# Cross attention with layer norm on one core: score products over stacked high and low parts of q

## The chip, the core and the metric

One NeuronCore of a Trainium2 chip runs the whole kernel. The metric is device time in microseconds (us); lower is better. TensorE (PE) has weight loads recorded apart from its products (PEld). The other engines are VectorE (DVE), ScalarE (ACT), GpSimd (POOL) and SyncE (SP), which here only issues DMAs.

## What is computed

x is 4 x 2048 x 512, the context 4 x 77 x 512, all float32, and there are 16 heads of 32.

```python
qs = (x @ wq) in heads;  ks, vs = (ctx @ wk), (ctx @ wv) in heads
scores = qs . ks / sqrt(32);  scores = where(mask, -inf, scores)
attn = softmax(scores) @ vs
out = attn @ wo + x
result = (out - mean) / sqrt(var + 1e-5) * gamma + beta
```

## The kernel before

The 8192 rows of x make 64 tiles t of 128 rows, and 16 blocks of 4 tiles. The weights, x and q are each split into a high part, rounded to fp32r by ScalarE's copy, and a low part, the rest. A product of two split numbers is made of three fp32r matmuls: high by high, high by low, low by high.

q is projected transposed, a block at a time and in four pieces of 128 columns of wq: `project_q(i)` gives, for block i // 4, the q of the four heads of group i % 4 (12 matmuls of 512 columns, line 287). ScalarE copies the high part out of PSUM into `qh` (`keep_q`), VectorE subtracts for the low part `ql` (`low_q`, line 579). `kh` and `kl` hold k as a block diagonal over four heads: 128 contraction rows (4 heads x 32) by 4 x 77 = 308 columns.

`scores(t, groups)` (line 303) makes for each of a tile's four groups three matmuls of 308 columns, which add up in one PSUM bank; stationary are `qh`, `qh`, `ql`, moving `kh`, `kl`, `kh`. `mask_max` (lines 591 and 597) adds the mask and takes the row maximum, `exps` (451) is ScalarE's exponential, `row_sums` (604, 606) VectorE's sum and reciprocal, `normalise` (742, 744) GpSimd's product, `transpose_p` (313, 315) turns the weights round on TensorE, `keep_pt` copies them out, `weigh_v` (335) multiplies with v once for two or four tiles, `keep_a` and `low_a` split the result, `project_o` (348) multiplies with wo (12 matmuls of 512 columns), and `residual`, `deviation`, `standardise` and `gain_and_shift` make the layer norm. `score` work of tile t and output work of tile t - 5 (`LAG`) share an iteration.

Each engine's program is written out in order by hand, and semaphores join them. TensorE's iteration t is: scores of groups 0 and 1; a projection (of o, or of q in the tiles in `SECOND`, t = 5, 9, 13 and so on, where `weigh_v` follows); the transposes of tile t - 1, first half; scores of groups 2 and 3; the other projection; in the tiles in `FIRST` a `weigh_v`; the transposes, second half. q(t + 4) is projected in iteration t. Each MATMUL of the program has a weight load of its own.

SyncE issues every DMA in one order: context, wk, wq and slices of x (`load_slice`; 64 slices of 256 KB through the three buffers of `xraw`), then wv, mask, slices, wo, the first residual tiles, gamma, beta, mask, slices. In iteration t it loads slice t + 10, places v at t = 1 and t = 3 (`place_v`, ten DMAs each, lines 205 and 209), stores tile t - 7 (242) and loads a residual tile (193). A wait of one of these holds up all behind it. Opening work of VectorE that matters: `low_k` makes `kl`, one group at a time.

## Time and profile before

| | |
|---|---|
| median of 3 runs | 662.82 us (661.82 to 666.81) |
| the profiled execution | 661.71 us, of which the span is 659.7 us |
| granted TensorE clock, mean over the span | 0.993 |
| busy share of the span | PE 96%, PEld 74%, DVE 81%, ACT 77%, POOL 74% |
| DMA | 57.78 MB, mean 88 GB/s |

The span runs from the first to the last instruction; the profiled execution's own time is 2.0 us longer than that. Matmuls are pipelined and the ends of their records are modelled, so a record of one lasts longer than the next one is away: the distance from start to start, or the piece in the chain divided by its count, is what one costs.

### The profile page before, as it was taken

To read this page: it belongs to the slowest core of one execution; us is meant where nothing else is said; L and a number is where in the kernel's file an instruction comes from. 1 tells how busy PE (TensorE), PEld (TensorE's weight loads), DVE (VectorE), ACT (ScalarE), POOL (GpSimd) and SP (SyncE) were. 2 spreads that over 40 slices of the span, in tenths; PEclk is the share of its full clock that TensorE was granted. 3 is DMA by queue.
4 is the path that set the end of the run, shared out by engine and by line. 5 is a ranking of instruction groups with operands and counts; after the bars stand their busy time and mean duration, and the time that the engine had idled before them with its cause. 6 is when DMAs were issued, how large, how long until landed. Compare 5 with 4: busy or idle time off the path is not lost.

```text
span 659.7 us, 13001 instructions
## 1 busy us (share of the span) xinstructions
PE 630.9 (96%) x4096; PEld 488.7 (74%) x4096; DVE 531.1 (81%) x1010; ACT 510.4 (77%) x1560; POOL 488.5 (74%) x631
## 2 busy tenths in 40 slices
PE   7979899999999999999999999999999999998883
PEld 5647687786878778687878778786877868785762
DVE  5766778788879878887888978887887988787886
ACT  4677888797887878797888879788887878788650
POOL 6334449696986969697896969698796969577663
PEclk9989999999999999999999999999999999999998
DMA  8542112221232313221232222122221222111214
GB/s 259 199 119 51 44 43 90 78 96 65 97 106 81 96 48 105 89 97 65 81 107 94 73 76 96 66 96 98 79 97 64 84 79 65 49 49 65 80 34 143
DMA packets 36563, 57.78 MB, mean 88 GB/s; under 512 B 8592, under 2 KB 9616, under 8 KB 36496
## 3 DMA queue, kind: packets, MB, share of 16 engines
q1 hardware_dynamic: 36496, 56.96, 25.8%
q8 instruction: 34, 0.56, 0.3%
q14 instruction: 33, 0.27, 0.1%
HBM read 39.53 MB, written 16.78 MB: 85 GB/s over the span
## 4 chain that ended last, share of the span: by engine, by line
PE 80%; DVE 10%; ACT 4%; DMA 2%; issue 2%; SPq 1%; POOL 1%; POOLq 0%; DVEq 0%; ACTq 0%
PE bank L348 23%; PE bank L287 23%; PE bank L303 14%; PE bank L313 8%; PE bank L335 8%; DMA xraw<-xT 2%; ACT pr L451 2%; PE bank L315 2%; DVE pr L591 2%; DVE sm L604 1%; DVE nm L597 1%; DVE st L625 1%; PE bank L271 1%; ACT kh L474 1%; DVE pf L570 1%
## 5 line engine op out<-in xcount | busy, mean ns | idle before, releaser
L451 ACT ACTIVATE pr<-pr,nm 128x77 f32<-128x77 f32 x1024 | 269.9, 347 | 70.9 <-DVE nm L597 70.2
L742 POOL TENSOR_TENSOR pn<-pr,rec 128x512 f32<-128x512 f32 x128 | 135.0, 1054 | 113.8 <-DVE rec L606 106.0
L591 DVE SCALAR_TENSOR_TENSOR pr<-msk,bank 128x308 f32<-128x308 uint8 x256 | 109.4, 468 | 44.4 <-PE bank L303 44.3
L604 DVE TENSOR_REDUCE sm<-pr 128x8 f32<-128x616 f32 x128 | 99.3, 776 | 11.2 <-ACT pr L451 11.0
L597 DVE TENSOR_REDUCE nm<-pr 128x8 f32<-128x616 f32 x128 | 101.8, 795 | 4.4
L287 PE MATMUL bank<-xh,wqh 128*128 128x512 f32 x256 | 102.6, 401 | 1.9 <-DVE ql L579 1.3
L348 PE MATMUL bank<-woh,ah 128*128 128x512 f32 x256 | 101.6, 397 | 0.1
L348 PE MATMUL bank<-woh,al 128*128 128x512 f32 x256 | 101.3, 396 | 0.0
L348 PE MATMUL bank<-wol,ah 128*128 128x512 f32 x256 | 101.1, 395 | 0.0
L287 PE MATMUL bank<-xh,wql 128*128 128x512 f32 x256 | 100.6, 393 | 0.0
L287 PE MATMUL bank<-xl,wqh 128*128 128x512 f32 x256 | 100.2, 392 | 0.0
L734 POOL TENSOR_TENSOR xl<-xraw,xh 128x512 fp32r<-128x512 f32 x64 | 83.6, 1309 | 20.8 <-ACT xh L420 20.8
L420 ACT ACTIVATE ptr<-bank 128x512 f32<-128x512 f32 (+1 forms) x256 | 95.5, 426 | 3.4 <-PE bank L313 3.4
L313 PEld LDWEIGHTS bank<-ident,pn 128*128 128x128 f32 x512 | 60.6, 140 | 48.7 <-issue 24.5
L303 PE MATMUL bank<-kh,qh 128*128 128x308 f32 x256 | 88.7, 346 | 1.5 <-DVE ql L579 0.9
L313 PE MATMUL bank<-ident,pn 128*128 128x128 f32 x512 | 78.7, 276 | 9.2 <-ACT ptr L420 5.9
L303 PE MATMUL bank<-kh,ql 128*128 128x308 f32 x256 | 78.1, 305 | 0.0
L303 PE MATMUL bank<-kl,qh 128*128 128x308 f32 x256 | 78.0, 305 | 0.0
L768 POOL TENSOR_TENSOR y<-y,bet 128x512 f32<-128x512 f32 x56 | 72.8, 1299 | 4.4
L766 POOL TENSOR_TENSOR y<-y,gam 128x512 f32<-128x512 f32 x56 | 72.5, 1294 | 0.0
L579 DVE TENSOR_TENSOR ql<-bank,qh 128x512 fp32r<-128x512 f32 x64 | 43.8, 684 | 32.7 <-ACT qh L420 32.6
L467 ACT ACTIVATE y<-z,rs 128x512 f32<-128x512 f32 x56 | 46.0, 821 | 22.7 <-POOL rs L761 22.3
(63 smaller groups left out, 1083.9 us busy)
## 6 DMA issues: line engine op xcount, KB each, us to landing
xraw<-xT SPq DMA_DIRECT2D x64, 256.0 KB, 3.0
xres<-x SPq DMA_DIRECT2D x64, 256.0 KB, 2.6
out<-y SPq DMA_DIRECT2D x56, 256.0 KB, 2.0
wk_sb<-wk SPq DMA_DIRECT2D x4, 256.0 KB, 4.6
wq_raw<-wq SPq DMA_DIRECT2D x4, 256.0 KB, 5.9
wv_sb<-wv SPq DMA_DIRECT2D x1, 1024.0 KB, 6.3
wo_raw<-wo SPq DMA_DIRECT2D x1, 1024.0 KB, 6.4
out<-wv_sb SPq DMA_DIRECT2D x4, 256.0 KB, 3.7
```

The lines of the kernel that those rows point to most:

```text
L287: last = nc.tensor.matmul(o[:], w[:, k, m * P:(m + 1) * P], s[:, blk % 2, k, :], start=(n == 0), stop=(n == 3 * KT - 1))
L303: last = nc.tensor.matmul(o, w[blk % 2][:, g, r * P:(r + 1) * P], s[:, g, t // TB, :], start=(n == 0), stop=(n == 2))
L313: last = nc.tensor.transpose(PTB[0][:, s * P:(s + 1) * P], pn[:, half, s, :], ident[:])
L348: last = nc.tensor.matmul(o[:], w[:, k, r * P:(r + 1) * P], s[:, k, :], start=(n == 0), stop=(n == 3 * KT - 1))
L420: return nc.scalar.activation(dst, src, ACT.Copy)
L451: last = nc.scalar.activation(s, s, ACT.Exp, bias=nm[:, t % 2, h:h + 1], scale=1.0)
L591: nc.vector.scalar_tensor_tensor(out=pr[:, 4 * g:4 * g + 4, :], in0=msk[:, b % 2, t % TB, :].unsqueeze(1).broadcast_to([P, 4, LK]), scalar ...
L597: nc.vector.tensor_reduce(nm[:, t % 2, HH * half:HH * half + HH], pr[:, HH * half:HH * half + HH, :], AX.X, ALU.max, negate=True).then_inc ...
L604: nc.vector.tensor_reduce(sm[:, t % 2, hs], pr[:, hs, :], AX.X, ALU.add).then_inc(v_sum, 1)
L734: nc.gpsimd.tensor_tensor(xl[:, n // KT % 2, n % KT, :], xraw[:, n % NX, :], xh[:, n // KT % 2, n % KT, :].bitcast(f32), ALU.subtract).the ...
L742: nc.gpsimd.tensor_tensor(pn[:, half, 0:4, :].rearrange("p s (e k) -> p (s e) k", e=2), pr[:, hs, 0:KM], rec[:, t % 2, hs].unsqueeze(2).br ...
L768: nc.gpsimd.tensor_tensor(y_of(o), y_of(o), bet[:], ALU.add).then_inc(g_y, 1)
```

## The change

The scores are formed for two heads at a time. The 128 contraction rows hold the high part of q for a pair of heads (64 rows) and its low part (64 rows), in the new tiles `qx`; `kh` and `kl` hold k for a pair (2 x 77 = 154 columns) in both halves of the rows. A group is then two pairs by (`kh`, `kl`), four matmuls of 154 columns, 616 in place of 3 x 308 = 924; low by low is now in the sum too. DMAs move the rows: `pair_k` copies k to the other half of the rows (8 DMAs once), `stack_q` puts the two parts of each q piece in place (4 DMAs of 64 rows x 2 KB for each of 64). ScalarE and VectorE write q's parts into two-slot buffers (`qth`, `qtl`; the first four pieces into `ptr`) and wait with piece i for the stacking of piece i - 2.

q is projected one piece earlier (`q_early`, `q_late`: q(t + 5) from t = 3 on). The first eight slices of x have buffers of their own; the wo load, the residual loads and the split of wo (now in four parts, iterations 1 to 4) come later; `project_v(0)` goes ahead of the first scores and `project_v(1)` between the two halves; ScalarE's `exps(0, 0)` goes ahead of its work on slice 8.

The diff, cut, with eight leading blanks of each line taken away:

```diff
+PW = 2 * LK
...
+def q_early(t):
+    return (7,) if t == 3 else (t + 5,) if t in SECOND else ()
+def q_late(t):
+    return () if t < 0 or t in SECOND or t >= T - 5 else (t + 4,) if t < 3 else (t + 5,)
...
-kh = sb("kh", [P, NG, NB, GW], f32r)
-kl = sb("kl", [P, NG, NB, GW], f32r)
+kh = sb("kh", [P, NG, 2, NB, PW], f32r)
+kl = sb("kl", [P, NG, 2, NB, PW], f32r)
...
 xraw = sb("xraw", [P, NX, D])
-xh = sb("xh", [P, 2, KT, D], f32r)
-xl = sb("xl", [P, 2, KT, D], f32r)
+with ExitStack() as split:
+    xh = split.enter_context(nc.sbuf_tensor("xh", [P, 2, KT, D], f32r))
+    xl = split.enter_context(nc.sbuf_tensor("xl", [P, 2, KT, D], f32r))
+zt = sb("zt", [P, 4 * KT, D])
...
 ptr = sb("ptr", [P, 2, 5, D])
+qth = sb("qth", [P, 2, D], f32r)
+qtl = sb("qtl", [P, 2, D], f32r)
+qx0 = sb("qx0", [P, NG, 2, D], f32r)
...
+qx1 = sb("qx1", [P, NG, 2, D], f32r)
...
-qh, ql = (qh0, qh1), (ql0, ql1)
...
+qx = (qx0, qx1)
+def x_of(n):
+    return (xraw[:, n] if n < NX else ptr[:, 0, 4, :] if n < KT else wo_raw[:, n - KT, :] if n < 2 * KT
+            else xraw[:, (n - 2 * KT) % NX])
+def x_arrived(n):
+    return (d_x[n], 16) if n < 2 * KT else (d_xt[(n - 2 * KT) % NX], 16 * ((n - 2 * KT) // NX + 1))
+def q_temp(i):
+    rows = (ptr[:, 0, i, :].bitcast(f32r), ptr[:, 1, i, :].bitcast(f32r)) if i < 4 else (qth[:, i % 2, :], qtl[:, i % 2, :])
+    return rows
 def z_of(o):
-    return z[:, o % 2] if o < VFIN else wv_sb[:, o - VFIN] if o < VFIN + KT else xraw[:, o - VFIN - KT]
+    return z[:, o % 2] if o < VFIN else zt[:, o - VFIN]
...
+d_kd, d_qx = [sem(f"d_kd{i}") for i in range(2)], [sem(f"d_qx{m}") for m in range(NG)]
+d_x = [sem(f"d_x{n}") for n in range(2 * KT)]
...
 misc = [("q", i) for i in range(4)]
 for t in range(T):
     o = [("o", t - LAG)] if t >= LAG else []
-    q = [("q", t + 4)] if t + 4 < T else []
-    misc += q + o if t in SECOND else o + q
+    misc += [("q", i) for i in q_early(t)]
+    misc += o if t not in SECOND else []
+    misc += [("q", i) for i in q_late(t)]
+    misc += o if t in SECOND else []
 misc += [("o", o) for o in range(T - LAG, T)]
...
     def load_slice(n):
-        if n >= NX:
-            sp.wait_ge(g_xl, n - NX + 1)
-        sp.dma_start(xraw[:, n % NX, :], xT[n // KT, :, n % KT, :]).then_inc(d_xt[n % NX], 16)
+        if n >= 2 * KT:
+            sp.wait_ge(g_xl, n - NX + 1 if n >= 2 * KT + NX else n - 2 * KT + 1)
+        sp.dma_start(x_of(n), xT[n // KT, :, n % KT, :]).then_inc(x_arrived(n)[0], 16)
...
+    def pair_k(g):
+        for k, done in ((kh, a_k), (kl, v_k)):
+            sp.wait_ge(done, 4 * g + 8)
+            for u in range(2):
+                here, there = slice(64 * u, 64 * u + 64), slice(64 - 64 * u, 128 - 64 * u)
+                sp.dma_start(k[there, g:g + 2, u].rearrange("p g b k -> p g (b k)").bitcast(f32),
+                             k[here, g:g + 2, u].rearrange("p g b k -> p g (b k)").bitcast(f32)
+                             ).then_inc(d_kd[g // 2], 16)
+    def stack_q(i):
+        blk, m = i // 4, i % 4
+        if blk >= 2:
+            sp.wait_ge(p_s, 4 * NG * (blk - 1))
+        sp.wait_ge(a_qh, i + 1)
+        for u in range(2):
+            rows = slice(64 * u, 64 * u + 64)
+            sp.dma_start(qx[blk % 2][rows, m, u].bitcast(f32), q_temp(i)[0][rows].bitcast(f32)).then_inc(d_qx[m], 16)
+        sp.wait_ge(v_ql, i + 1)
+        for u in range(2):
+            here, there = slice(64 * u, 64 * u + 64), slice(64 - 64 * u, 128 - 64 * u)
+            sp.dma_start(qx[blk % 2][there, m, u].bitcast(f32), q_temp(i)[1][here].bitcast(f32)).then_inc(d_qx[m], 16)
     for k in range(KT):
         sp.dma_start(wq_raw[:, k, :], w_v(wq)[:, k, :]).then_inc(d_wq[k], 16)
         load_slice(k)
     sp.dma_start(wv_sb[:], w_v(wv)).then_inc(d_wv, 16)
-    load_mask(0)
     for n in range(4, 8):
         load_slice(n)
+    load_mask(0)
+    pair_k(0)
+    stack_q(0)
+    stack_q(1)
+    pair_k(2)
+    stack_q(2)
+    stack_q(3)
+    load_mask(1)
+    for n in range(8, 11):
+        load_slice(n)
+    sp.wait_ge(g_xl, 2 * KT)
     sp.dma_start(wo_raw[:], w_v(wo)).then_inc(d_wo, 16)
-    for t in range(XR):
-        load_res(t)
     sp.dma_start(gam[:], gamma.partition_broadcast(P)).then_inc(d_gb, 16)
     sp.dma_start(bet[:], beta.partition_broadcast(P)).then_inc(d_gb, 16)
-    load_mask(1)
-    for n in range(8, 10):
-        load_slice(n)
     for t in range(T + 3):
-        if t + 10 < 4 * NBLK:
-            load_slice(t + 10)
+        for i in q_late(t - 1) + q_early(t):
+            stack_q(i)
+        if t + 11 < 4 * NBLK:
+            load_slice(t + 11)
         if t == 1:
...
             sp.wait_ge(a_v, NB)
             place_v(1, NB, d_vm[1])
+            for r in range(XR):
+                load_res(r)
...
             if t == 0:
-                pe.wait_ge(v_k, 4 * g + 4)
-            pe.wait_ge(v_ql, 4 * blk + g + 1)
+                pe.wait_ge(d_kd[g // 2], 64)
+            pe.wait_ge(d_qx[g], 64 * (blk + 1))
             if i >= 2:
                 pe.wait_ge(v_st, i - 1)
-            o = SB[i % 2][:, 0:GW]
-            for n, (w, s) in enumerate(((qh, kh), (qh, kl), (ql, kh))):
-                last = nc.tensor.matmul(o, w[blk % 2][:, g, r * P:(r + 1) * P], s[:, g, t // TB, :],
-                                        start=(n == 0), stop=(n == 2))
+            for u in range(2):
+                for k in (kh, kl):
+                    last = nc.tensor.matmul(SB[i % 2][:, u * PW:(u + 1) * PW],
+                                            qx[blk % 2][:, g, u, r * P:(r + 1) * P], k[:, g, u, t // TB, :],
+                                            start=(k is kh), stop=(k is kl))
             last.then_inc(p_s, 1)
...
     for t in range(T - 4):
-        scores(t, (0, 1))
         if t == 0:
             project_v(0)
+        scores(t, (0, 1))
+        if t < 3:
+            project_v(t + 1)
         if t == 1:
             pe.wait_ge(g_id, 2)
+        for i in q_early(t):
+            project_q(i)
         if t in SECOND:
-            project_q(t + 4)
             weigh_v(SECOND[t])
         elif t >= LAG:
             project_o(t - LAG)
         if t >= 1:
             transpose_p(t - 1, 0)
         scores(t, (2, 3))
-        if t < 3:
-            project_v(t + 1)
+        for i in q_late(t):
+            project_q(i)
         if t in SECOND:
             if t == LAG:
-                pe.wait_ge(a_w, KT + 1)
-                pe.wait_ge(v_w, KT + 1)
+                pe.wait_ge(a_w, 2 * KT)
+                pe.wait_ge(v_w, 2 * KT)
             project_o(t - LAG)
-        else:
-            project_q(t + 4)
         if t in FIRST:
             weigh_v(FIRST[t])
...
     def keep_x(n):
-        act.wait_ge(d_xt[n % NX], 16 * (n // NX + 1))
+        act.wait_ge(*x_arrived(n))
         if n // KT >= 2:
             act.wait_ge(p_q, 4 * (n // KT - 1))
-        keep(xh[:, n // KT % 2, n % KT, :], xraw[:, n % NX, :]).then_inc(a_xh, 1)
+        keep(xh[:, n // KT % 2, n % KT, :], x_of(n)).then_inc(a_xh, 1)
     def keep_q(i):
-        blk, m = i // 4, i % 4
         act.wait_ge(p_q, i + 1)
-        if i == 4:
-            act.wait_ge(v_w, KT)
-        if blk >= 2:
-            act.wait_ge(p_s, 4 * NG * (blk - 1))
-        keep(qh[blk % 2][:, m, :], misc_bank(("q", i))[:]).then_inc(a_qh, 1)
+        if i >= 6:
+            act.wait_ge(v_ql, i - 1)
+            act.wait_ge(d_qx[(i - 2) % 4], 64 * ((i - 2) // 4 + 1))
+        keep(q_temp(i)[0], misc_bank(("q", i))[:]).then_inc(a_qh, 1)
...
-            nc.scalar.activation(kh[rows, g, :, j * LK:(j + 1) * LK],
+            nc.scalar.activation(kh[rows, g, j // 2, :, j % 2 * LK:(j % 2 + 1) * LK],
...
-    for n in range(5, 8):
+    keep_x(5)
+    keep_q(3)
+    for n in range(6, 8):
         keep_x(n)
-    keep_q(3)
-    act.wait_ge(d_wo, 16)
-    keep(woh[:], wo_raw[:]).then_inc(a_w, 1)
     for t in range(T - 4):
-        if t >= 1 and t - 1 not in SECOND:
-            keep_q(t + 3)
+        for i in q_late(t - 1):
+            keep_q(i)
         if t - 1 in FIRST:
             keep_a(FIRST[t - 1])
         if t >= 2:
             keep_pt(t - 2, 1)
-        if t + 8 < 4 * NBLK:
-            keep_x(t + 8)
+        if t == 0:
+            keep_v(0)
+            exps(0, 0)
+            keep_x(8)
+        if t + 9 < 4 * NBLK:
+            keep_x(t + 9)
         if t > LAG:
             standardise(t - LAG - 1)
-        exps(t, 0)
+        if t == 1:
+            act.wait_ge(d_wo, 16)
+        if 1 <= t <= KT:
+            keep(woh[:, t - 1, :], wo_raw[:, t - 1, :]).then_inc(a_w, 1)
+        if t >= 1:
+            exps(t, 0)
         if t < 3:
-            keep_v(t)
+            keep_v(t + 1)
+        for i in q_early(t):
+            keep_q(i)
         if t in SECOND:
-            keep_q(t + 4)
             keep_a(SECOND[t])
         if t >= 1:
             keep_pt(t - 1, 0)
-        if t == 2:
-            keep_v(3)
         exps(t, 1)
...
         ts = slice(b * TB, (b + 1) * TB)
+        if b == 0:
+            dve.wait_ge(p_v, NB)
         nc.vector.tensor_reduce(pf[:, 0], msk[:, b % 2], AX.X, ALU.min).then_inc(v_pf, 1)
...
     def low_q(i):
-        blk, m = i // 4, i % 4
         dve.wait_ge(a_qh, i + 1)
-        nc.vector.tensor_tensor(ql[blk % 2][:, m, :], misc_bank(("q", i))[:],
-                                qh[blk % 2][:, m, :].bitcast(f32), ALU.subtract).then_inc(v_ql, 1)
+        if i >= 6:
+            dve.wait_ge(d_qx[(i - 2) % 4], 64 * ((i - 2) // 4 + 1))
+        nc.vector.tensor_tensor(q_temp(i)[1], misc_bank(("q", i))[:], q_temp(i)[0].bitcast(f32),
+                                ALU.subtract).then_inc(v_ql, 1)
...
         mask_max(t, 0)
-        if t == 0:
-            dve.wait_ge(a_w, KT + 1)
-            nc.vector.tensor_tensor(wol[:], wo_raw[:], woh[:].bitcast(f32), ALU.subtract).then_inc(v_w, 1)
-        if t >= 1 and t - 1 not in SECOND:
-            low_q(t + 3)
+        if 1 <= t <= KT:
+            dve.wait_ge(a_w, KT + t)
+            nc.vector.tensor_tensor(wol[:, t - 1, :], wo_raw[:, t - 1, :], woh[:, t - 1, :].bitcast(f32),
+                                    ALU.subtract).then_inc(v_w, 1)
+        for i in q_late(t - 1) + q_early(t):
+            low_q(i)
         if t in SECOND:
-            low_q(t + 4)
             low_a(SECOND[t])
...
-    for n in range(8):
+    for n in range(9):
         low_x(n)
...
-        if t + 8 < 4 * NBLK:
-            low_x(t + 8)
+        if t + 9 < 4 * NBLK:
+            low_x(t + 9)
         normalise(t, 0)
```

## Rows read from the trace of the kernel before

**Rows 1.** Page: busy time and instructions, then the granted clock in 40 slices

```profile
PE 630.9 (96%) x4096; PEld 488.7 (74%) x4096; DVE 531.1 (81%) x1010; ACT 510.4 (77%) x1560; POOL 488.5 (74%) x631
...
PEclk9989999999999999999999999999999999999998
```

**Rows 2.** Windows: stretch, length, busy PE, PEld, DVE, ACT, POOL, PEclk, DMA share, GB/s

```profile
30.00:80.00 50.00, 43.80 (x223) 29.56 (x222) 33.95 (x61) 36.41 (x115) 21.26 (x26) 0.97 0.32 92
80.00:600.00 520.00, 518.68 (x3415) 410.36 (x3414) 430.81 (x838) 428.54 (x1322) 416.70 (x545) 1.00 0.24 81
301.78:339.10 37.32, 37.32 (x249) 29.61 (x248) 30.69 (x61) 31.12 (x97) 30.79 (x41) 1.00 0.24 86
```

**Rows 3.** Chain that ended last, 301 to 340 us: start, us, what

```profile
308.01 1.88 PE bank L335 x32
...
311.44 2.81 PE bank L348 x12
314.24 0.44 PE bank L313 x4
314.68 0.11 PE bank L315
...
318.99 0.85 PE bank L303 x6
319.83 2.77 PE bank L287 x12
```

**Rows 4.** Groups by form, weight loads of the scores with equal weights

```profile
L303 PEld LDWEIGHTS bank<-kl,qh 128*128 128x128 f32 x256 | 48.9, 191 | 0.1
L303 PEld LDWEIGHTS bank<-kh,qh 128*128 128x128 f32 x256 | 48.7, 190 | 3.9 <-issue 2.6 <-DVE ql L579 1.1
```

**Rows 5.** Timeline of PEld, after a stall and after transposes

```profile
21.40 0.19 PEld L287 LDWEIGHTS bank<-xh,wqh 128*128 128x128 f32 x1 [0.45 <-DVE ql L579]
21.51 0.19 PEld L287 LDWEIGHTS bank<-xl,wqh 128*128 128x128 f32 x1
21.75 0.19 PEld L287 LDWEIGHTS bank<-xh,wql 128*128 128x128 f32 x1
...
88.92 0.19 PEld L303 LDWEIGHTS bank<-kh,qh 128*128 128x128 f32 x1
89.03 0.19 PEld L303 LDWEIGHTS bank<-kl,qh 128*128 128x128 f32 x1
89.17 0.19 PEld L303 LDWEIGHTS bank<-kh,ql 128*128 128x128 f32 x1
```

**Rows 6.** Groups by form: the float32 products of v

```profile
L271 PE MATMUL bank<-wv_sb,ctx_sb 128*77 128x512 f32 x32 | 14.8, 606 | 0.0
```

**Rows 7.** Chain that ended last, opening

```profile
30.30 7.12 DMA xraw<-xT
37.43 0.02 issue
37.45 0.63 ACT xh L420
38.09 1.30 ACT pr L451 x6
...
55.69 3.43 PE bank L271 x8
...
76.23 1.88 PE bank L335 x32
```

**Rows 8.** Timeline of PE, opening: idle, then half clock

```profile
42.80 0.63 PE L313 MATMUL bank<-ident,pn 128*128 128x128 f32 x4 [3.10 <-POOL pn L744]
...
44.55 0.46 PE L303 MATMUL bank<-kl,qh 128*128 128x308 f32 x1
44.81 0.46 PE L303 MATMUL bank<-kh,ql 128*128 128x308 f32 x1
```

**Rows 9.** Timeline of SP's queue: v placed, and a steady store

```profile
59.78 0.68 SPq L205 DMA_DIRECT2D vm<-vs  x1
60.50 3.80 SPq L209 DMA_DIRECT2D vr<-vs  x4
...
329.56 0.34 SPq L242 DMA_DIRECT2D out<-y  x1
```

**Rows 10.** Timeline of DVE, steady stretch: low part of a q piece

```profile
326.12 0.68 DVE L579 TENSOR_TENSOR ql<-bank,qh 128x512 fp32r<-128x512 f32 x1
```

**Rows 11.** Page: DMA issues, KB each, median us to landing

```profile
xraw<-xT SPq DMA_DIRECT2D x64, 256.0 KB, 3.0
out<-y SPq DMA_DIRECT2D x56, 256.0 KB, 2.0
```

## Prediction before the run

> **What bounds the kernel now.** I read the page first. The reader is to see that TensorE is busy for 96% of the span and that 4096 products stand beside 4096 weight loads [rows 1], so each product has a load of its own. The windows then say where TensorE is the bound [rows 2]: from 80 to 600 us it is busy for 518.68 of 520.00 us, at the full clock (2.4 GHz), while VectorE has 430.81. From 30 to 80 us it is idle for 50.00 - 43.80 = 6.2 us. One round of four tiles, 301.78 to 339.10, is 37.32 us, all of it TensorE's; VectorE and ScalarE have 30.69 and 31.12. The chain of waits in that stretch holds nothing but TensorE's own pieces [rows 3]: twelve products of 512 columns in 2.77 or 2.81 us, the six score products of half a tile in 0.85, five transposes in 0.44 + 0.11, and the products with v in 1.88. So in 520 us of the 660, whatever a TensorE instruction gains or loses is the kernel's. That stretch has 520 / 37.32 x 16 = 223 of the 256 groups of scores.
>
> **Score products in the long stretch.** Now a product of 308 columns costs 0.85 / 6 = 0.142 us, a group 0.426. Full clock takes 308 / 2.4 = 0.128 for the columns alone, 0.014 less. A product of 512 columns costs 2.77 / 12 = 0.231, where the columns take 0.213. Through these two points a column costs 0.00044 us, and a product of 154 columns would be 0.142 - 154 x 0.00044 = 0.075 us. Four of these are 0.30 a group, 0.126 less than now. This is the low end.
>
> But each of the four has a load of 128 rows by 128 columns before it, and that nothing skips a load where the weights are the same is seen in the two groups of loads with the stationary `qh`: 256 each, 191 and 190 ns [rows 4]. These durations overlap in a stream; what one load keeps the next waiting is seen where no product is in the way [rows 5]. After a stall the loads start at 21.40, 21.51 and 21.75: the second starts 0.11 after the first, when the first has left its place, the third 0.24 later, a whole 512-column product. After the transposes it is 88.92, 89.03, 89.17: 0.11, and then 0.14, a 308-column product. So a product can't follow its forerunner by less than its load needs, 0.11 us, and at 154 columns the load is the longer of the two (0.11 against 0.075). The four products of a group then cost 4 x 0.11 = 0.44, not 0.30, and 0.426 before: fewer columns, and a little more time.
>
> The Trainium skill says the same from its side: "TensorE: Matmul & The Clock Gate", section "LDWEIGHTS (loading the stationary operand)", gives a load as its columns over 1.2 GHz whatever its rows, 107 ns for 128, and the section on weight-path perf modes leaves float32 out of the fast load. By that 107 ns alone the group would be 0.43 us, and the stretch 0 to 1 us longer. The rows of the loads agree, at 0.11.
>
> The high end for a load-bound product is the load plus the same 0.014 by which a 308-column product exceeds what its columns need: 0.124, a group 0.496. I take 0.113, near the row: products of fp32r all run somewhat over what their columns need, and I don't know that this part vanishes. The group is then 0.452, and the stretch grows by 0.026 x 223 = 5.8 us (3.1 at 0.11, 15.6 at 0.124; -28 at the low end). The 33 groups outside the stretch are beside waits of other engines; I give them nothing.
>
> **Other engines, steady.** VectorE, ScalarE and GpSimd have the same operations on the same sizes. The stacking adds 4 x 64 DMAs of 128 KB, 33.5 MB, to 57.8. The engines of the DMA are 0.24 busy in the stretch [rows 2], so the traffic lies beside the rest. SyncE issues four more in each tile of 8.4 to 9.3 us, at 0.34 to 0.7 us each [rows 9], behind the wait for the low part and ahead of the slice, the store and the residual tile. What is it late for? The low part of the last piece of a block is done at 326.80 [rows 10]; two DMAs behind it (0.9) and 3.0 us to landing, the slower row [rows 11], give 330.7. That piece is of group 3, so what reads it is the second half of the scores of the tile after next, at 335.7 in this stretch (326.12 + 9.6, a tile and its `weigh_v` on); 5.0 us to spare. The store at 329.56 comes after the four issues would be over (328.6). I cost both at nothing; if the cover is gone the price is that of rival three. ScalarE's and VectorE's new wait, with piece i for the landing of piece i - 2, looks back a whole tile or more: nothing. The high part of a piece waits no longer on the scores of a block; SyncE does.
>
> **Opening.** Now the chain there runs through SyncE's queue into slice 8 of x (7.12 us), ScalarE's copy of it, and only then the first exponentials at 38.09 [rows 7]. TensorE idles 3.10 us before its first transposes and then runs at half clock for a stretch: 0.26 us for 308 columns, 1.2 GHz [rows 8]. The change takes that chain away. With the same durations: the fourth q piece ends at 27.0, `project_v(0)` to 30.5 (eight records in 3.43 [rows 7]); by then k's copies and the first two pieces, issued from 20.6 to 25, have landed, for they need 3.0 us. Scores, mask and maximum bring the first exponentials to 32.9, 5.2 us sooner. `project_v(1)`, though, now lies ahead of the scores of groups 2 and 3 (35.9 for 32.6). Adding up TensorE's own pieces from there gives the first `weigh_v` at 71.0, with one q piece (2.77) more behind it than the `weigh_v` of now, at 76.23. What is late then is v itself. SyncE places it at t = 3 by ten DMAs: 0.68 for one and 3.80 for four [rows 9], 9.0 us in all. These now stand behind the stacking of q(7), whose low part I get at 63.6; four issues and a slice bring the placing to 66 at most and 64.7 at best, its end to 74, its landing to about 76. `weigh_v` starts then, as before, but with the extra q piece done: 2.8 us gained, less about 1 us of half clock after an idle time of 5 us, as in rows 8. I take -2. At the one end, all idle time of 30 to 80 us and the half-clock loss go: -8. At the other, the longer queue of SyncE (8 DMAs of k, 16 of q) holds the first scores or v by one more round of such issues: +4.
>
> The extra piece is taken from the end, where TensorE isn't the bound; it counts in the long stretch, and it is in the 2.8. The split of wo in four parts costs ScalarE and VectorE under 1 us more than now, beside TensorE.
>
> **Sum.** The profiled execution is 661.7 us (span 659.7, 2.0 around it). 661.7 + 5.8 - 2 = 665.5, which is 0.4% over the median of 662.8, whose runs spread by 5 us. A measurement of this kernel can tell about 1% from no change, that is below 656.2 or above 669.4.
>
> **Rivals.**
> 1. *The columns decide.* If a load hides more than rows 5 show (the load of equal weights, say), a group is 0.30: 0.126 x 223 = 28 us less; VectorE, 6.6 us free in each 37.32, lets all of it through. 661.7 - 28 - 2 = 632. For it: every steady fp32r product of the trace is paced by its columns. Against it: the 0.11 between two loads.
> 2. *Narrow fp32r products are slow.* The trace has none under 308 columns. A float32 product of v takes two records (32 for 16 products [rows 6]) of 3.43 / 8 = 0.43 us at 512 columns, four times what fp32r needs. If fp32r below some width fell back to that, 154 columns would be 0.26 us and a group 1.03: 0.61 x 256 = 155 us more, 815. It ends on the other side at once, from the first group on. For it only that nothing excludes it; against it that 308 and 512 columns lie on one line of cost.
> 3. *The stacking comes late.* If at each of 15 block starts TensorE waits for the last piece, 1.5 us each, the time is 665.5 + 22 = 688. It decides from the point where issue to landing takes over 3.0 + 5.0 = 8 us: the rows have 2 to 3 us.
> 4. *The opening alone decides.* Loads at 0.11 and all of the opening's idle time gone: 661.7 + 3.1 - 8 = 657, which can't be told from no change.
>
> **Numbers.** Loads pace the products (my forecast, rival 4 within it): 72%, of its own from 657 to 679 (low 3.1 and -8, high 15.6 and +2). Columns decide: 15%. Slow narrow products: 6%. Late stacking: 7%. The range reaches from 650, for loads partly hidden, to 681. Faster by over 1%: rival 1 and 4 points of the forecast's low edge, 0.19. Slower by over 1%: rivals 2 and 3, and 20 points of the forecast (0.12 us a product and up), 0.33. Within 1%: 0.48.
>
> **What the profile after would show.** 1024 score products and loads where 768 were (4352 in all). In the chain of a steady stretch eight of them in 0.88 to 0.93 us; 0.60 would be rival 1, 2.1 rival 2. Four tiles in 37.4 to 38.2 us. The starts of loads within a group 0.11 apart, now set by the load and not the product. TensorE idle at the first scores of a block, with a DMA as releaser, is rival 3. In the opening the first exponentials near 33 us, and the first `weigh_v` waiting for a DMA of v. My forecast is wrong if the round of four tiles gets shorter than 37.0 us, or if a wait that isn't TensorE's own enters its chain between 80 and 600 us.

## The result, and the profile after

The changed kernel takes 678.84 us, median of 4 runs (678.11 to 679.49), against 662.32 before: the ratio is 1.0237, 95% interval 1.0196 to 1.0278. That is 16.5 us slower. The forecast was 665.5 us with a range from 650 to 681, so the range holds the time; but the likeliest case was "within 1%", at 0.48, and slower by over 1% had 0.33. The profiled execution has a span of 677.5 us, 17.8 more than the 659.7 of before.

The page of the changed kernel, busy time and granted clock, answers to [rows 1]:

```profile
PE 643.1 (95%) x4352; PEld 499.5 (74%) x4352; DVE 535.9 (79%) x1013; ACT 511.0 (75%) x1563; POOL 487.3 (72%) x631
...
PEclk9979889999999999999999999999999999998998
```

The 256 more products with their 256 loads are there. The granted clock is down in three of the first six slices, where it was in one. The windows of the changed kernel answer to [rows 2]; columns as there:

```profile
30.00:80.00 50.00, 42.30 (x199) 30.42 (x198) 30.03 (x53) 30.64 (x95) 18.53 (x23) 0.90 0.67 170
80.00:600.00 520.00, 515.41 (x3589) 405.91 (x3588) 424.70 (x821) 419.81 (x1293) 403.38 (x528) 1.00 0.49 136
```

The DMA engines' share has doubled, 0.24 to 0.49, in the long stretch. TensorE still fills it, but for one wait that ends at 87.09 us, which the chain explains below. The prediction named such a wait between 80 and 600 us as a sign that its forecast is wrong. Between 30 and 80 us it is idle longer than before (7.7 for 6.2 us) and at a mean clock of 0.90.

The chain that ended last, in the steady stretch of the changed kernel, answers to [rows 3]; columns are start, us, what:

```profile
304.71 0.85 PE bank L368 x8
305.57 2.84 PE bank L352 x12
```

Eight products of 154 columns have the 0.85 us that six of 308 had: 0.106 us each in this view, whose pieces are cut at the modelled ends of the records (forecast 0.88 to 0.93). The loads tell it better; PEld's timeline of the changed kernel answers to [rows 5]:

```profile
304.44 0.19 PEld L368 LDWEIGHTS bank<-kh,qx 128*128 128x128 f32 x1
304.55 0.19 PEld L368 LDWEIGHTS bank<-kl,qx 128*128 128x128 f32 x1
...
305.33 0.19 PEld L352 LDWEIGHTS bank<-xh,wqh 128*128 128x128 f32 x1
305.45 0.19 PEld L352 LDWEIGHTS bank<-xl,wqh 128*128 128x128 f32 x1
```

Eight loads in 305.33 - 304.44 = 0.89 us, 0.111 each, evenly. Product follows product at the pace of the loads; the projection after them goes back to the pace of its 512 columns.

How much this costs is read between two places that both kernels have, the second product with v (tile 5) and the one thirteen rounds of four tiles later. From the chain, before and after:

```profile
82.42 1.88 PE bank L335 x32
...
571.85 1.88 PE bank L335 x32
```

```profile
95.05 1.88 PE bank L401 x32
...
589.77 1.88 PE bank L401 x32
```

Before: 571.85 - 82.42 = 489.43, 37.65 us a round. After: 494.72, 38.06 a round. The long stretch has grown by 5.3 us. What lies ahead of it has grown by 95.05 - 82.42 = 12.6 us. What lies behind is the same, 87.7 for 87.9 us. 12.6 + 5.3 - 0.1 = 17.8. So the larger part of the loss is in the first 95 us.

There the chain of the changed kernel is no longer TensorE's:

```profile
30.17 0.91 SPq L250
31.12 6.07 DMA kl<-kl
37.19 2.32 issue
39.51 0.65 PE bank L368 x4
...
72.07 0.69 DVE qtl L653
...
77.13 0.64 SPq L237
...
84.99 2.02 DMA vr<-vs
...
87.09 2.86 PE bank L401 x32
```

Two things are to be seen. The last copy of k is issued at 31.12 and lands 6.07 us later, at 37.19, but the scores of groups 2 and 3 of tile 0 start only at 39.51 and 41.79. What they still lack are the stacked pieces q(2) and q(3), whose DMAs stand behind that copy: by the trace's semaphore events the last of q(2) lands at 39.42 and the last of q(3) at 41.70, each 0.1 us before the scores. The profile puts these two waits down to "issue". And the first product with v waits for v, which SyncE places from 77.13 on, after the stacking of q(6) and q(7); the low part of q(6) (L653) is made only from 72.07 to 72.76. The waits of TensorE up to 98 us (waited for: us in total, times, longest):

```profile
PE bank L368 <- issue: 5.5, 2, 3.8
...
PE bank L401 <- DMA vr<-vs: 3.7, 1, 3.7
```

So v is the smaller part. TensorE had come to its first product with v at 87.09 - 3.7 = 83.4 us, where it started at 76.23 before.

The timeline of SyncE's queue in the changed kernel shows the row of copies, 0.6 us for most and up to 1.35 for some; slices 8 to 10 of x, which stand behind them, are issued from 39.22 on. ScalarE then sits idle for slice 8 until 42.81:

```profile
34.75 1.23 SPq L266 DMA_DIRECT2D qx<-ptr  x2
...
37.31 1.24 SPq L266 DMA_DIRECT2D qx<-ptr  x2
...
39.22 1.39 SPq L220 DMA_DIRECT2D xraw<-xT  x3
```

```profile
42.81 1.28 ACT L487 ACTIVATE xh<-xraw 128x512 fp32r<-128x512 f32 x2 [7.09 <-DMA xraw<-xT]
```

### The profile page after: what moved, and what is told of

Its sections match the earlier page's. It is cut to its first block, busy times and chain, and to the rows that moved or that the text cites. A ratio compares the mean times of both kernels' runs of the same rounds, so it can differ in the third digit from the quotient of the medians.

```text
span 677.5 us, 13898 instructions
## 1 busy us (share of the span) xinstructions
PE 643.1 (95%) x4352; PEld 499.5 (74%) x4352; DVE 535.9 (79%) x1013; ACT 511.0 (75%) x1563; POOL 487.3 (72%) x631
## 4 chain that ended last, share of the span: by engine, by line
PE 79%; DVE 8%; SPq 4%; issue 3%; DMA 2%; ACT 2%; POOL 1%; POOLq 0%; DVEq 0%; ACTq 0%
PE bank L352 24%; PE bank L414 23%; PE bank L368 14%; PE bank L401 8%; PE bank L379 8%; PE bank L381 2%; DVE pr L665 2%; DVE sm L678 1%; DVE st L699 1%; ACT pr L516 1%; PE bank L336 1%; DVE nm L671 1%; DMA xraw<-xT 1%; SPq L241 1%; DMA kl<-kl 1%
## 5 line engine op out<-in xcount | busy, mean ns | idle before, releaser
L368 PE MATMUL bank<-kh,qx 128*128 128x154 f32 x512 | 127.9, 288 | 5.7 <-issue 5.5
L368 PE MATMUL bank<-kl,qx 128*128 128x154 f32 x512 | 121.8, 276 | 0.0
L352 PE MATMUL bank<-xh,wqh 128*128 128x512 f32 x256 | 105.5, 412 | 3.5 <-DVE qtl L653 2.8
L368 PEld LDWEIGHTS bank<-kh,qx 128*128 128x128 f32 x512 | 99.0, 193 | 8.0 <-issue 7.9
L414 PE MATMUL bank<-woh,ah 128*128 128x512 f32 x256 | 103.8, 405 | 0.0
L352 PE MATMUL bank<-xl,wqh 128*128 128x512 f32 x256 | 102.4, 400 | 0.0
L487 ACT ACTIVATE ptr<-bank 128x128 f32<-128x128 f32 (+2 forms) x260 | 97.8, 428 | 5.7 <-PE bank L379 3.4
L368 PEld LDWEIGHTS bank<-kl,qx 128*128 128x128 f32 x512 | 99.0, 193 | 0.3 <-issue 0.2
L807 POOL TENSOR_TENSOR xl<-xraw,xh 128x512 fp32r<-128x512 f32 x59 | 76.9, 1305 | 18.9 <-ACT xh L487 18.9
L653 DVE TENSOR_TENSOR qtl<-bank,qth 128x512 fp32r<-128x512 f32 x60 | 41.0, 684 | 29.3 <-ACT qth L487 29.3
```

The costliest lines, as they stand in the source:

```text
L352: last = nc.tensor.matmul(o[:], w[:, k, m * P:(m + 1) * P], s[:, blk % 2, k, :], start=(n == 0), stop=(n == 3 * KT - 1))
L368: last = nc.tensor.matmul(SB[i % 2][:, u * PW:(u + 1) * PW], qx[blk % 2][:, g, u, r * P:(r + 1) * P], k[:, g, u, t // TB, :], start=(k is ...
L414: last = nc.tensor.matmul(o[:], w[:, k, r * P:(r + 1) * P], s[:, k, :], start=(n == 0), stop=(n == 3 * KT - 1))
L487: return nc.scalar.activation(dst, src, ACT.Copy)
L807: nc.gpsimd.tensor_tensor(xl[:, n // KT % 2, n % KT, :], x_of(n), xh[:, n // KT % 2, n % KT, :].bitcast(f32), ALU.subtract).then_inc(g_xl, 1)
```

## The experiments

Times are medians; ratios are to the kernel before on the same chip, where this had 662.4, 663.37 and 662.93 us in the three sets of runs. So differences of medians from different sets carry about 1 us of doubt. "Round" is the mean of the same thirteen rounds of four tiles.

**Narrow products alone.** The kernel before with this edit; the low part of q is left out of the scores.

```diff
-                    for n, (w, s) in enumerate(((qh, kh), (qh, kl), (ql, kh))):
+                    for u in range(2):
+                        cols = slice(u * GW // 2, (u + 1) * GW // 2)
+                        for k in (kh, kl):
...
```

> The kernel before, with four score products of 154 columns a group (high part of q by the high and the low part of k, each in two halves of columns) in place of three of 308; low part of q by k is left out. No copy, no new order. If the weight loads pace narrow products (0.112 us each), eight of them take 0.90 us where six took 0.85, a round of four tiles grows from 37.5 to 37.9 us and the time is 662.3 + 6 = 668 us. If columns paced them, 634 us. If the longer rounds of the changed kernel come from the traffic of the copies, 662 us.

Measured: 670.27 us, ratio 1.0113 (1.0074 to 1.0152). From the chain of this run:

```profile
86.87 1.88 PE bank L336 x32
...
580.20 1.88 PE bank L336 x32
```

493.33 us, 37.95 a round, 0.30 more than before: 3.9 of the 5.3 us without a single copy. Fewer columns (616 for 924) and a longer time: columns don't decide. It lost a further 4.5 us up to tile 5 (86.87 for 82.42), which I had not expected; see the last run.

**The change with wide products.** All of the changed kernel, but three products of 308 columns on its tiles; parts of the sum are left out.

```diff
-                    for u in range(2):
-                        for k in (kh, kl):
+                    for n, (u, k) in enumerate(((0, kh), (0, kl), (1, kh))):
...
```

> The changed kernel with its copies, waits and order, but three score products of 308 columns a group on the same tiles; the sum leaves out some of the parts. If loads pace the narrow products, the rounds go back from 37.9 to 37.5 us and the time from 678.8 to 673 us, the opening as late as in the changed kernel. If copies or their traffic lengthen the rounds, these stay at 37.9 and the time at 679 us.

Measured: 675.66 us, ratio 1.019 (1.0157 to 1.0223), 3.2 us under the changed kernel. Its chain has the two products with v at

```profile
94.32 1.88 PE bank L400 x32
...
585.87 1.88 PE bank L400 x32
```

37.81 us a round, 0.25 less than the changed kernel; the opening is late as ever. The direction is that of the loads, the size under what I wrote (673 us and 37.5 a round). The next run has wide products in the same order and no copies, with 37.75 us a round, so most of what is left over 37.65 comes with the order and not with the copies.

**The order alone.** No copies of k, no stacking: ScalarE and VectorE write the parts of q straight into the tile that the scores read, and the products are the three of before. The order of all engines, the buffers of x and the split of wo are the changed kernel's.

```diff
-            pair_k(0)
-            stack_q(0)
...
-                for i in q_late(t - 1) + q_early(t):
-                    stack_q(i)
...
         def q_temp(i):
+            return qx[i // 4 % 2][:, i % 4, 0, :], qx[i // 4 % 2][:, i % 4, 1, :]
```

> The changed kernel's order, buffers of x and split of wo, but no stacking and no copies of k: q's parts go straight to their tiles and the scores are three products of 308 columns, as before. If the 13 us lost in the opening are the copies in the queue of SyncE and on the DMA engines, the first product with v comes at 77 us or sooner, one piece of q ahead, and the time is 655 to 660 us. If the new order itself loses them, the time is 672 us or more.

Measured: 661.02 us over 10 runs, ratio 0.9966 (0.9948 to 0.9984). The new order doesn't lose the 12.6 us, the copies do; but it gains 1.4, where I had expected 2 to 7. Its chain shows why:

```profile
57.14 2.81 PE bank L342 x12
...
60.03 0.63 ACT xh L475
...
80.13 1.88 PE bank L389 x32
...
570.88 1.88 PE bank L389 x32
```

ScalarE rounds slice 12 in tile 3 now (60.03). The buffer for it is free when q(7) is projected, and that ends at 59.95; the exponentials of tile 3 are queued behind. Before, slice 12 was a tile later. TensorE then waits 1.9 us at 63.22 for VectorE's low part of q, and its granted clock falls to half for a part of what follows (mean 0.83 from 60 to 70 us). So a wait of the new order takes back part of what the first exponentials had gained: the second product with v is 2.3 us sooner than before. A round is 37.75 us.

**v ahead of two stackings.** The changed kernel, with the second placing of v issued ahead of the stacking of q(6) and q(7).

```diff
+                if t == 3:
+                    sp.wait_ge(a_v, NB)
+                    place_v(1, NB, d_vm[1])
                 for i in q_late(t - 1) + q_early(t):
                     stack_q(i)
```

> The changed kernel with the second placing of v issued ahead of the stacking of pieces 6 and 7. In the changed kernel TensorE waits 3.7 us for v at 87 us. If SyncE's order makes that wait, it goes, and the time falls by 3 to 4 us to 675 us, unless the pieces stacked 9 us later hold up the scores of tile 4; then it stays at 679 us or grows.

Measured: 678.49 us, ratio 1.0229 (1.0196 to 1.0263): no difference from the changed kernel. The chain of this run:

```profile
74.12 0.81 SPq L241
...
76.83 2.32 DMA qx<-qtl
...
79.75 0.77 ACT ptr L488 x2
```

v's last DMA is now issued at 74.12 for 84.99, and piece 6 of q is late in its turn. ScalarE may write piece 8 only when piece 6 has landed, 79.15 us, and its copies of the transposes stand behind that wait. The second product with v comes at 92.96 us, 2.1 sooner, of which the profiled span keeps 1.2. The two kinds of DMA are on one queue, and what one gains in it the other loses.

**Without the copies of k.** Eight DMAs fewer; k's second half of rows stays zero, so q's low part is left out.

```diff
-            pair_k(0)
...
-            pair_k(2)
...
-                        pe.wait_ge(d_kd[g // 2], 64)
+                        pe.wait_ge(v_k, 4 * g + 4)
```

> The changed kernel without its eight copies of k (the second half of k's rows stays zero, so the part with q's low half is left out). The copies of k take 0.6 to 1.2 us each of SyncE's queue, 7 us in all, and have the longest landing times (4 to 6 us). If they hold up the opening, the scores of groups 2 and 3 of tile 0, at 39.5 and 41.8 us in the changed kernel, come before 37 us, slice 8 and the placing of v come up to 5 us sooner, and the time is 673 to 675 us. If it is the 4 x 64 copies of q alone, the time stays at 678 us.

Measured: 670.88 us, ratio 1.0109 (1.0089 to 1.0128), 8.0 us under the changed kernel and more than I had written. Chain:

```profile
34.80 0.85 PE bank L366 x8
...
85.91 1.88 PE bank L399 x32
...
580.65 1.88 PE bank L399 x32
```

The scores of groups 2 and 3 of tile 0 start at 34.80, where PE's order has them, not at 39.51. The second product with v moves by 9.1 us. A round is 38.06 us, that of the changed kernel. Three things go together here. The last DMA that stacks one of the first four pieces is issued 8.4 us sooner, and slice 8 at 30.79 for 39.22. The DMAs that stack the first four pieces land in 2.2 to 2.4 us, where they took 3.3 to 5.3 beside k's copies (DMA share 0.99 from 20 to 30 us, against 0.78 without them). And TensorE, which no longer idles at 36 to 42 us, keeps its full clock there: the windows from 30 to 90 us lose 10 x (0.34 + 0.17 + 0.10) = 6.1 us of full clock in the changed kernel and 10 x (0.04 + 0.13) = 1.7 without k's copies, as many as before the change. By this estimate up to 4.4 of the 8.0 us are clock. This run doesn't part the place in the queue from the load on the DMA engines.

**Idle copies.** The order-only kernel with all 256 copies of q issued in SyncE's queue where the stackings stand, into buffers that nothing reads.

```diff
+            for i in range(4):
+                idle_copy(i)
...
+                for i in q_late(t - 1) + q_early(t):
+                    idle_copy(i)
                 if t + 11 < 4 * NBLK:
```

> The order-only kernel (wide products, parts of q written in place, 661.0 us) with the 4 x 64 copies of q issued all the same, at the stackings' places in SyncE's queue, into buffers that nothing reads; no k copies. TensorE waits for none of them. If the queue of SyncE and the traffic of the copies hold up the opening (slices of x, v), the first product with v moves from 74.5 to 80 us or more and the time to 668 to 672 us. If it is TensorE's waits for the landings, the time stays at 661 to 662 us. The rounds of four tiles, 37.75 us, show whether the traffic itself costs in the long stretch: 37.75 if not.

Measured: 666.48 us, ratio 1.0046 (1.0028 to 1.0064), 5.5 over the order-only kernel. Chain:

```profile
62.83 0.61 DVE qx L660
...
68.12 0.63 SPq L236
...
78.16 3.67 PE bank L406 x32
...
86.78 1.88 PE bank L406 x32
...
577.81 1.88 PE bank L406 x32
```

TensorE waits for none of these copies (SyncE, ScalarE and VectorE do, for the landing of one two pieces or more back), and yet the first product with v comes at 78.16, after 4.1 us of waiting for v; it was at 73.83 in the order-only kernel. It is their place in the queue: SyncE waits for the low part of q(6), made at 62.83, issues the copies of q(6) and q(7), and only at 68.12 the first DMA of v, which the order-only kernel issues at 52.92. In the long stretch a round is 37.77 us for 37.75, with the DMA share at 0.49 for 0.24: the traffic costs nothing there.

**Widths.** The kernel before with another width of the score products in each of the four batches; what lies beyond is left out.

```diff
+                    wide = (GW, 256, 200, 128)[t // TB]
+                    o = SB[i % 2][:, 0:wide]
```

> The kernel before, whose three score products of a group have 308 columns in the first batch, 256 in the second, 200 in the third and 128 in the fourth (what lies beyond is left out). If the load of 0.112 us paces narrow products, six of them take 0.85 us at 308 columns, 0.71 at 256, 0.67 at 200 and 0.67 at 128, with loads 0.112 apart from 200 down; the time is about 3 x 14 x 8 x 0.02 = 8 us less, 650 to 656 us. If columns paced them, 0.41 us at 128 and 640 us or less. If narrow fp32r products fell to the rate of float32, over 1.4 us and 700 us or more.

Measured: 649.6 us over 2 runs, ratio 0.9792 (0.9766 to 0.9818), just under the 650 to 656 expected. From its chain, batches of 256, 200 and 128 columns, then PEld's timeline at 128:

```profile
202.18 0.71 PE bank L304 x6
...
385.85 0.66 PE bank L304 x6
...
521.42 0.62 PE bank L304 x6
```

```profile
521.15 0.19 PEld L304 LDWEIGHTS bank<-kh,qh 128*128 128x128 f32 x1
...
521.82 0.19 PEld L287 LDWEIGHTS bank<-xh,wqh 128*128 128x128 f32 x1
```

Six loads take 0.67 us at 128 columns, 0.112 each, where columns alone would take 128 / 2.4 = 0.053. From 308 to 256 columns the piece of six shrinks by 0.14 us, from 200 to 128 by 0.04. So the pace goes over from columns to loads between 256 columns (0.118 us a product) and 200 (0.110). The run also excludes a slow rate of narrow fp32r products.

**First exponentials ahead.** The kernel before; only the order of tile 0 is mended (GpSimd's `normalise(0, 0)` goes ahead of its work on slice 8 too, VectorE's split of wo behind the first row sums).

```diff
             keep_q(3)
+            keep_v(0)
+            exps(0, 0)
             act.wait_ge(d_wo, 16)
...
+                if t == 0:
+                    exps(0, 1)
                 if t + 8 < 4 * NBLK:
                     keep_x(t + 8)
```

> The kernel before with nothing but the opening's order mended: the exponentials and the normalising of tile 0 go ahead of the work on slice 8 of x and of the split of wo. If the 7 us of waiting for that slice are what idles TensorE at 40 us, the first transposes come at 36 to 38 us for 42.8, no half clock follows, and the time is 656 to 659 us. If the next waits (v, the exponentials of tile 3) take it back, 661 to 662 us.

Measured: 657.58 us, ratio 0.9917 (0.99 to 0.9934). This version is faster than both kernels, by 0.8% than the one before. The first transposes no longer wait for slice 8, and the stretch at half clock that followed is gone: the product after them, at 40.98, lasts 0.30 us where it had 0.46 in [rows 8]. PE's timeline:

```profile
39.72 0.62 PE L313 MATMUL bank<-ident,pn 128*128 128x128 f32 x4
...
40.98 0.30 PE L303 MATMUL bank<-kl,qh 128*128 128x308 f32 x1
```

The transposes come at 39.72, not at the 36 to 38 us that I had expected, and without a wait. In [rows 8] TensorE idled 3.10 us before 42.80, so its own pieces last until 39.70 in either kernel.

**Split of wo in parts, later.** On top of the run before this.

```diff
+                if t < KT:
+                    keep(woh[:, t, :], wo_raw[:, t, :]).then_inc(a_w, 1)
```

> The kernel of the run with the first exponentials ahead, with the split of wo in four parts, one in each of tiles 0 to 3, behind the work on the slices, where the one piece (1.8 us on ScalarE, 2.5 on VectorE) stood in the chain at 35 to 39 us. If that piece sets the first transposes (40.3 us), they come at 37 to 38 us and the time falls by 1 to 2 us more, to 656 us. If the later waits (exponentials of tile 3, 60 to 68 us) set the pace anyway, 657.6 us.

Measured: 658.78 us, ratio 0.9944 (0.9921 to 0.9967), no gain and perhaps a loss of 1. The split's first part now waits behind ScalarE's work on slice 8, and that DMA is back in the chain, as `30.53 7.29 DMA xraw<-xT`. My premise was wrong as well: in the run before, the transposes waited for nothing, so the split of wo didn't set them. Here the scores behind them wait 1.02 us, where they waited 0.32.

**Narrow from tile 5 on.** The first experiment again, with wide products in tiles 0 to 4.

```diff
+                    parts = 1 if t < 5 else 2
+                    for u in range(parts):
```

> The kernel before with products of 154 columns from tile 5 on only (as in the first run, low part of q left out there); tiles 0 to 4 have the three products of 308. The first run lost 4 us in the rounds and 4.6 us in the opening, where two stretches at half clock stood for one. If narrow products bring on the second stretch, this kernel has only the rounds' 4 us: 666 to 667.5 us, granted clock about 0.99. If the second stretch is a matter of its own, or the 4.6 us come otherwise, 670 us and 0.984.

Measured: 667.87 us, ratio 1.0078 (1.0051 to 1.0105). Rounds of 37.95 us again:

```profile
84.36 1.88 PE bank L341 x32
...
577.72 1.88 PE bank L341 x32
```

The windows 40 to 50 and 70 to 80 us, first of the narrow kernel, then of this one (columns as in [rows 2]):

```profile
40.00:50.00 10.00, 6.94 (x21) 4.04 (x21) 6.70 (x13) 8.31 (x30) 5.02 (x6) 0.66 0.19 43
...
70.00:80.00 10.00, 7.57 (x33) 6.33 (x32) 6.54 (x13) 7.67 (x27) 5.16 (x7) 0.67 0.20 55
```

```profile
40.00:50.00 10.00, 6.92 (x20) 3.92 (x19) 6.70 (x13) 8.30 (x30) 5.01 (x7) 0.66 0.19 43
...
70.00:80.00 10.00, 7.58 (x65) 4.94 (x64) 6.71 (x13) 8.29 (x29) 5.36 (x7) 1.00 0.18 55
```

The stretch at half clock between 70 and 80 us is gone with the narrow products of the opening, and the median is 2.4 us lower; 667.87 is just over the 666 to 667.5 expected. TensorE's waits around 73 us are the same in both (1.5 and 0.9 us). The mean granted clocks of all runs point the same way: 0.982 to 0.988 in four runs of the narrow kernel, 0.989 to 0.993 in four of this one (the kernel before had 0.986 to 0.994 beside the one and 0.986 to 0.996 beside the other). So in every run narrow products in tiles 0 to 4 go with less granted clock; how they bring it about is open. The other part of the 4.5 us, the 1.9 by which this kernel is behind the one before at tile 5, isn't due to them: between 40 and 50 us the clock is 0.66 here and 0.83 in the profile of the kernel before, 1.7 us of full clock, and the kernel before has the same program up to tile 5. That is a difference between executions.

## Why the prediction was right and wrong, point by point

**The pace of narrow products: right.** The load sets it, 0.111 us between loads where I took 0.113. The stretch grew by 5.3 us in 13 rounds, where 0.026 x 16 x 13 = 5.4 was forecast. That the two are so close is in part luck: 3.9 belong to the narrow products by themselves (0.30 x 13), or 3.2 by the run with wide products, and the rest to what the kernel otherwise changed. The order-only kernel has 0.10 us a round more than before, which I can't tell apart further. The Trainium skill ("TensorE: Matmul & The Clock Gate", "LDWEIGHTS (loading the stationary operand)") gives the time of a load as its columns over 1.2 GHz; for 128 columns that is an estimate of 107 ns. The measured 0.111 and 0.112 in two kernels are near it at full clock. At half clock they aren't: the loads of the changed kernel at 41.92, 42.14 and 42.36 us are 0.22 apart, and the measurement decides. Rivals 1 and 2 are excluded by the run of widths.

**Copies beside the long stretch: right.** Rounds of 37.77 for 37.75 us with idle copies at the same DMA share; behind the opening TensorE waited for no stacked piece. Rival 3, a wait at each start of a block, didn't happen; the stacked pieces were late in the opening alone (0.2, 3.8 and 1.6 us).

**The opening: wrong.** I took -2, with 4 at the worst; the second product with v came 12.6 us later. The first exponentials did come near the forecast (33.62 for 32.9), but what stood behind them did not. The failed step is the sentence that k's copies and the first pieces, "issued from 20.6 to 25, have landed" by 30.5, and the one that gave the end of v's placing as 74. It failed in three of its terms.
1. The sentence has time for one of the two `pair_k` and two pieces of q, and none for the second `pair_k` and the third and fourth piece behind it. SyncE issued 24 DMAs from 19.0 to 38.5 us, 18.6 us of issuing or 0.77 each, where I worked with 0.45. The last copy of k left at 31.12 and took 6.07 us, not 3.0; q(2) and q(3), queued behind it, landed at 39.42 and 41.70, and TensorE waited 5.5 us for them. Half clock followed, as in [rows 8] but for longer (granted clock 0.66 from 40 to 50 us for 0.83). Slice 8 left at 39.22, and ScalarE's wait for it is in the profile again, though not in the chain. Without k's copies the time is 8.0 us less.
2. v is placed behind the stacking of q(7), as I wrote; but the low part of q(7), which I had at 63.6, was done at 73.97, and that of q(6) at 72.8. The placing began at 77.13 and not at 66, and ended near 86 and not at 74. In tile 3 ScalarE's work on slice 12 waits for q(7) to be projected; its part of the split of wo stands behind that, VectorE's part behind ScalarE's, and the low part of q(6) behind that. I had costed these moves one by one, as busy time, and not their order. The copies of q, even idle ones, cost 5.5 us by their place in the queue.
3. "Looks back a whole tile or more: nothing", of the wait with piece i for piece i - 2: true in the order as it is, but with v moved ahead it became the chain. What seemed two independent costs is one queue.

So the range held the time by luck. With the load cost that was measured and the opening at its worst it gives 661.7 + 5.3 + 4 = 671; it reached 681 only for loads far slower than they are.

The parts add up: 662.4, less 1.4 for the order, 5.5 for q's copies, 8.0 for k's, and 3.2 to 3.9 for the narrow products give 677.7 to 678.4, measured 678.84. Three of these are steps from one kernel to the next, so the only test in the sum is the step that is left, from the idle copies to the changed kernel without k's: 4.4 us, where the narrow products explain 3.2 to 3.9.

**The piece of q taken from the end: wrong.** I counted 2.8 us for it. What lies behind the last round is as long as before (87.7 and 87.9 us), and as before the chain behind them runs for the most part through VectorE and ScalarE, in this kernel from 609.81 us on, 20.0 us after the last of these products, and in the one before from 600.04 on, 28.2 us after it.

**Rival 4** (the opening's idle time gone) asked for something that this change didn't do. The kernel before with only the calls for tile 0 moved gains 5.8 us of the 8 that the rival had. That its 657.58 us is close to the rival's 657 is chance: that sum has 3.1 us for narrow products in it, and this kernel has none.

## What to carry to other kernels

Count loads before columns: a product can't follow faster than its stationary tile is loaded, here 0.11 us for 128 columns at full clock, and four narrow products cost more than three wide ones. Where DMAs are added to a queue that is issued in order, write down that queue's schedule in full, with every instruction's issue time, and see what stands behind it, before any landing time is compared. Where the profile names no releaser ("issue"), look up the semaphores that the program waits for at that place. And a wait that the chain shows in an opening is worth a try by itself: moving the first exponentials ahead of the wait for slice 8 gained 0.8%.

## What the runs showed that I had not expected

- In the opening most issues of a copy of 64 rows (128 KB) took 0.59 to 0.62 us of SyncE's queue, some up to 1.16; most issues of a 256 KB load took 0.33 to 0.59. The smaller transfer isn't the cheaper one to issue. Eight copies of k, 308 KB each, took a median of 4.2 (`kh`) and 5.6 us (`kl`) to land; in the steady stretch a copy of 128 KB took 2.3.
- After an idle time of about 3 us TensorE's granted clock was at its lower level for a part of the same 10 us window that differed between runs of the same opening (mean 0.83 in one, 0.66 in another).
- At half clock the loads of narrow products start 0.22 us apart (41.92, 42.14, 42.36 us in the changed kernel), twice the 0.11 at full clock, where the 154 columns would need 154 / 1.2 = 0.128. So loads pace narrow products at either clock.
- Twelve products of 512 columns took from 2.75 to 2.84 us in kernels whose instructions there are the same. I know no cause.
